# The second layer of a mixture of experts as three products of split fp32r operands

## The reference

```python
xt = x.reshape(-1, d)                       # 4096 tokens, d = 256
route_prob = softmax(xt @ Wr + br)          # 8 experts
routes = argmax(route_prob)
for e in range(8):                          # a token keeps the result of its own expert
    h = gelu(xt @ W1[e] + b1[e])            # 256 -> 1024, exact GELU
    y = h @ W2[e] + b2[e]                   # 1024 -> 256
    out += y * (routes == e)[:, None]
```

## Time and profile before

| | us |
|---|---|
| median of 3 runs | 1250.32 |
| the three runs | 1249.89, 1250.32, 1256.76 |
| span of the profiled execution, first to last instruction | 1249.6 |
| TensorE busy (products) | 1141.2 |
| VectorE, ScalarE, GpSimd busy | 665.9, 424.2, 570.6 |

### The profile page before, as it was taken

One profiled execution on the slowest core, in us unless ns is written; L12 is line 12 of the kernel. 1 busy time (PEld: TensorE's weight loads), 2 busy tenths in 40 slices (PEclk: granted clock), 3 DMA queues, 4 the chain that ended last, 5 costly groups with the idle time before them and its releaser, 6 DMA issues. The chain is left out here.

```text
span 1249.6 us, 23166 instructions
## 1 busy us (share of the span) xinstructions
PE 1141.2 (91%) x7476; PEld 811.9 (65%) x7477; DVE 665.9 (53%) x1481; ACT 424.2 (34%) x501; POOL 570.6 (46%) x565
## 2 busy tenths in 40 slices
PE   6899999897679999999999999998726999999995
PEld 3577677575345555555555555556615999999994
DVE  3264636444557777777777777734751333333331
ACT  1302231311115555555555555563520111111110
POOL 0003030110217888888877787860262444444443
PEclk8899999898689999999999999998957999999998
DMA  7204351304151223232232323233445556556551
GB/s 208 60 1 126 129 175 61 126 34 168 68 188 41 94 64 102 71 98 77 76 92 60 93 59 93 60 119 113 160 113 181 192 195 214 189 192 214 194 191 61
DMA packets 61607, 148.42 MB, mean 119 GB/s; under 512 B 11360, under 2 KB 31776, under 8 KB 59904
## 3 DMA queue, kind: packets, MB, share of 16 engines
q1 hardware_dynamic: 53184, 123.39, 31.0%
q0 software_dynamic: 7536, 22.96, 5.7%
q10 hardware_dynamic: 848, 1.58, 0.5%
HBM read 104.58 MB, written 39.87 MB: 116 GB/s over the span
## 5 line engine op out<-in xcount | busy, mean ns | idle before, releaser
L217 DVE TENSOR_REDUCE s_nmax<-ps_v 128x1 f32<-128x512 f32 x484 | 311.5, 685 | 114.5 <-PE ps_v L211 104.6
L923 POOL TENSOR_TENSOR h_added<-h_added,h_expd 128x1024 f32<-128x1024 f32 x124 | 295.5, 2383 | 37.5 <-ACT h_expd L946 29.6
L946 ACT ACTIVATE h_expd<-ps_v 128x1024 f32<-128x1024 f32 x128 | 131.2, 1025 | 154.9 <-PE ps_v L972 150.3
L1669 PEld LDWEIGHTS ps_h<-xs_c,lnt 128*128 128x128 f32 x1248 | 148.0, 195 | 4.8 <-issue 2.9
L1669 PE MATMUL ps_h<-xs_c,lnt 128*128 128x128 f32 x1248 | 148.4, 278 | 2.3 <-DVE xs_c L1621 2.3
L1679 PE MATMUL ps_y<-w,vals_t 128*128 x624 | 141.2, 379 | 0.6 <-DVE ys L1634 0.6
L418 POOL TENSOR_TENSOR a_res<-a_res,a_lnt 128x2048 f32<-128x2048 f32 x4 | 18.2, 4538 | 266.2 <-DVE a_lnt L123 266.2
L986 PE MATMUL h_ps_o<-h_expd,s_vh 128*32 128x256 f32 x2048 | 137.2, 385 | 0.0
L946 ACT ACTIVATE h_expd<-h_ps_e 128x1024 f32<-128x1024 f32 x128 | 130.3, 1018 | 0.0
L580 PE MATMUL a_ps_v<-a_val,a_expd 128*128 128x257 f32 x512 | 123.4, 396 | 5.1 <-ACT a_expd L458 4.5
L1710 ACT ACTIVATE vals_t<-ps_h 128x1024 f32<-128x1024 f32 x39 | 39.9, 1024 | 255.6 <-DVE ps_h L1614 255.6
(11 more groups left out here) (208 smaller groups left out, 1530.5 us busy)
## 6 DMA issues: line engine op xcount, KB each, us to landing
lnt<-in_w SPq DMA_DIRECT2D x38, 1024.0 KB, 4.9
qk_scr<-a_head_hi SPq DMA_DIRECT2D x16, 512.0 KB, 2.7
qk_scr<-a_head_lo SPq DMA_DIRECT2D x16, 512.0 KB, 3.6
w<-in_w SPq DMA_DIRECT2D x8, 1024.0 KB, 5.5
xs<-xs_scr SPq DMA_DIRECT2D x39, 128.5 KB, 2.1
a_x_t<-in_x_t POOLq DMA_DIRECT2D x4, 1024.0 KB, 9.8
r_scr<-a_res POOLq DMA_DIRECT2D x4, 1024.0 KB, 5.5
v_scr<-res SPq DMA_DIRECT2D x4, 1024.0 KB, 3.9
```

The costliest lines, as they stand in the source:

```text
L217: self.nc.vector.tensor_reduce(self.nmax[k][:, nb, half:half + 1], ps_m[:, half, :], AX.X, ALU.max, negate=True).then_inc(self.v_max, 1)
L923: nc.gpsimd.tensor_tensor(total[:, :], (expd[:, 0, :] if m == 1 else total[:, :]), expd[:, m, :], ALU.add).then_inc(g_add, 1)
L946: nc.scalar.activation(expd[:, m, :], flat(ps_e[m % 2]), ACT.Exp, scale=SCALE).then_inc(a_exp, 1)
L1669: last = nc.tensor.matmul(ps_h[k][:, c // 4, c % 4 * P:(c % 4 + 1) * P], w1_now[k][:, t, c * P:(c + 1) * P], xs_c[:, t, :], start=(t == 0) ...
```

## The change

Only the expert stage computes differently. The units (GELU's outputs) and the second layer's weights are each split into a part rounded to fp32r and the rest, also of type fp32r. The second layer is then three products for each of 8 blocks: rounded units by rounded weights, rounded units by the weights' rest, and, last, the units' rest by the rounded weights; the product of the two rests is left out. These are 24 fp32r products with 256 columns in place of 8 fp32 products.

The new steps are: ScalarE rounds the units (Copy of 128 × 1024, right behind GELU) and the weights of the tile's expert (Copy of 128 × 2048, two tiles ahead); VectorE subtracts to get the weights' rest (128 × 2048, one tile ahead, behind the bias) and the units' rest (128 × 1024, behind the result). ScalarE also takes over the token copy from VectorE. TensorE reads the split weights at fixed places, so it no longer loads the expert's number; VectorE and ScalarE load it once more a tile. The wait for the second layer's weights moves from TensorE to ScalarE. New buffers (`hid_t`, `hids`, `w2s`) need room, so some that end with the routing stage are allocated so that they can be freed.

```diff
--- before.py
+++ after.py
@@ -1419,7 +1419,9 @@
 
         w1_now = [keep["lnt"][:, :, :].rearrange("p t c -> p (t c)")[:, k * CT * H:(k + 1) * CT * H].rearrange("p (t h) -> p t h", h=H)
                   for k in range(2)]
-        hid_t = [keep["vals_t"][:, k, :, :] for k in range(2)]
+        hid_t = [sb(f"hid_t{k}", [P, KC, P]) for k in range(2)]
+        hids = [[sb(f"hid_{x}{k}", [P, KC, P], F32R) for x in ("hi", "lo")] for k in range(2)]
+        w2s = [[sb(f"w2_{x}{k}", [P, KC, C], F32R) for x in ("hi", "lo")] for k in range(2)]
         ys = sb("ys", [P, C])
 
 
@@ -1436,9 +1438,9 @@
         g_pause, padded = sem("g_pause"), sem("padded")
         v_step, v_pad, v_start = sem("v_step2"), sem("v_pad"), sem("v_start")
         w1_in = [sem(f"w1_in{k}") for k in range(2)]
-        v_experts, v_xs, v_biased, v_rows, v_ys = sem("v_experts"), sem("v_xs"), sem("v_biased"), sem("v_rows"), sem("v_ys")
+        v_experts, v_biased, v_rows, v_ys = sem("v_experts"), sem("v_biased"), sem("v_rows"), sem("v_ys")
         pe_xs, pe_hid, pe_ys = sem("pe_xs"), sem("pe_hid"), sem("pe_ys")
-        a_gelu = sem("a_gelu")
+        a_gelu, a_xs, a_hid, a_w2, v_hid, v_w2 = (sem(n) for n in ("a_gelu", "a_xs", "a_hid", "a_w2", "v_hid", "v_w2"))
 
         all_consts = 16 * len(TABLE_CONSTS)
 
@@ -1615,10 +1617,20 @@
                                             b1_t[:, bass.ds(e, 1), :].rearrange("p o (k n) -> p (o k) n", n=1).to_broadcast([P, KC, P]),
                                             ALU.add).then_inc(v_biased, 1)
 
-                def tokens(i):
-
-                    dve.wait_ge(pe_xs, i + 1)
-                    nc.vector.tensor_copy(xs_c[:, :, :], ps_x[:, 0:C].rearrange("p (t n) -> p t n", t=CT)).then_inc(v_xs, 1)
+                def weights_lo(i, k):
+
+                    e = expert(i)
+                    dve.wait_ge(a_w2, i + 1)
+                    nc.vector.tensor_tensor(w2s[k][1][:, :, :].rearrange("p k n -> p (k n)"),
+                                            w2[:, bass.ds(e, 1), :, :].rearrange("p o k n -> p (o k n)"),
+                                            raw(w2s[k][0][:, :, :].rearrange("p k n -> p (k n)")), ALU.subtract).then_inc(v_w2, 1)
+
+                def units_lo(i, k):
+
+                    dve.wait_ge(a_hid, i + 1)
+                    nc.vector.tensor_tensor(hids[k][1][:, :, :].rearrange("p k n -> p (k n)"),
+                                            hid_t[k][:, :, :].rearrange("p k n -> p (k n)"),
+                                            raw(hids[k][0][:, :, :].rearrange("p k n -> p (k n)")), ALU.subtract).then_inc(v_hid, 1)
 
                 def result(i, first=False):
 
@@ -1636,21 +1648,21 @@
                 def tile(i, parity=0, first=False, next_tile=True, ahead=True):
                     if next_tile:
                         biased(i + 1, 1 - parity)
-                    if ahead:
-                        tokens(i + 2)
+                        weights_lo(i + 1, 1 - parity)
                     result(i, first)
+                    if next_tile:
+                        units_lo(i + 1, 1 - parity)
 
                 dve.wait_ge(v_experts, 1)
                 dve.wait_ge(bias_in, 32)
-                tokens(0)
+                weights_lo(0, 0)
                 biased(0, 0)
-                tokens(1)
+                units_lo(0, 0)
                 tiles(dve, tile)
 
             @block.tensor
             def _(pe):
                 pe.wait_ge(consts_in, all_consts)
-                pe.wait_ge(sems["w_in"], 16 * E)
 
                 def tokens(i):
                     pe.wait_ge(xs_in, 16 * i + 16)
@@ -1663,7 +1675,7 @@
                     pe.wait_ge(w1_in[k], 16 * nth)
                     if not first:
                         pe.wait_ge(a_gelu, i - 1)
-                    pe.wait_ge(v_xs, i + 1)
+                    pe.wait_ge(a_xs, i + 1)
                     for c in range(KC):
                         for t in range(CT):
                             last = nc.tensor.matmul(ps_h[k][:, c // 4, c % 4 * P:(c % 4 + 1) * P], w1_now[k][:, t, c * P:(c + 1) * P],
@@ -1671,14 +1683,16 @@
                     last.then_inc(pe_hid, 1)
 
                 def second_layer(i, k, first=False):
-                    e = pe.value_load(texp_i[0:1, bass.ds(i, 1)], min_val=0, max_val=E - 1)
                     if not first:
                         pe.wait_ge(v_ys, i)
-                    pe.wait_ge(a_gelu, i + 1)
+                    pe.wait_ge(a_hid, i + 1)
+                    pe.wait_ge(v_w2, i + 1)
                     for c in range(KC):
-                        last = nc.tensor.matmul(ps_y[:, 0:C], hid_t[k][:, c, :],
-                                                w2[:, bass.ds(e, 1), c, :].rearrange("p o n -> p (o n)"),
-                                                start=(c == 0), stop=(c == KC - 1))
+                        for part in range(2):
+                            nc.tensor.matmul(ps_y[:, 0:C], hids[k][0][:, c, :], w2s[k][part][:, c, :], start=(c + part == 0), stop=False)
+                    pe.wait_ge(v_hid, i + 1)
+                    for c in range(KC):
+                        last = nc.tensor.matmul(ps_y[:, 0:C], hids[k][1][:, c, :], w2s[k][0][:, c, :], start=False, stop=(c == KC - 1))
                     last.then_inc(pe_ys, 1)
 
                 def tile(i, parity=0, nth=1, first=False, next_tile=True, ahead=True):
@@ -1707,17 +1721,43 @@
                     if not first:
 
                         act.wait_ge(pe_ys, i - 1)
-                    nc.scalar.activation(hid_t[k].rearrange("p k n -> p (k n)"), flat(ps_h[k]), ACT.Gelu).then_inc(a_gelu, 1)
+                    nc.scalar.activation(hid_t[k][:, :, :].rearrange("p k n -> p (k n)"), flat(ps_h[k]), ACT.Gelu).then_inc(a_gelu, 1)
+                    act.wait_ge(a_gelu, i + 1)
+                    nc.scalar.activation(hids[k][0][:, :, :].rearrange("p k n -> p (k n)"),
+                                         hid_t[k][:, :, :].rearrange("p k n -> p (k n)"), ACT.Copy).then_inc(a_hid, 1)
+
+                def tokens(i):
+
+                    act.wait_ge(pe_xs, i + 1)
+                    nc.scalar.activation(xs_c[:, :, :].rearrange("p t n -> p (t n)"), ps_x[:, 0:C], ACT.Copy).then_inc(a_xs, 1)
+
+                def weights_hi(i, k, first=False):
+
+                    e = act.value_load(texp_i[0:1, bass.ds(i, 1)], min_val=0, max_val=E - 1)
+                    if not first:
+
+                        act.wait_ge(pe_ys, i - 1)
+                    nc.scalar.activation(w2s[k][0][:, :, :].rearrange("p k n -> p (k n)"),
+                                         w2[:, bass.ds(e, 1), :, :].rearrange("p o k n -> p (o k n)"), ACT.Copy).then_inc(a_w2, 1)
 
                 def tile(i, parity=0, first=False, next_tile=True, ahead=True):
+                    if ahead:
+                        tokens(i + 2)
                     if next_tile:
                         gelu(i + 1, 1 - parity, first)
+                    if ahead:
+                        weights_hi(i + 2, parity)
 
                 pad_rows(act, range(E // 2, E))
                 act.wait_ge(scattered, 16 * (TB - NB))
                 act.wait_ge(v_experts, 1)
                 e0 = act.value_load(texp_i[0:1, 0:1], min_val=0, max_val=E - 1)
                 act.dma_start(w1_now[0], io["w1"][bass.ds(e0, 1)].rearrange("o (t p) m -> p (o t) m", p=P)).then_inc(w1_in[0], 16)
+                act.wait_ge(sems["w_in"], 16 * E)
+                weights_hi(0, 0, first=True)
+                weights_hi(1, 1, first=True)
+                tokens(0)
+                tokens(1)
                 gelu(0, 0, first=True)
                 tiles(act, tile)
 
@@ -1738,18 +1778,19 @@
...
-        keep["token_id"] = ctx.enter_context(nc.sbuf_tensor("token_id", [P, TB], I32))
+        for n, shape in (("vals_t", [P, B * CT, NB, P]), ("res1", [P, NB, C]), ("vals_c", [P, CT, N])):
+            keep[n] = until_experts.enter_context(nc.sbuf_tensor(n, shape, F32))
         head_phase(nc, io, keep, sems, heads)
         during_heads.close()
-        keep.update(kept((("lnt", [P, TB, C + 1]),)))
-        keep["pos"] = ctx.enter_context(nc.sbuf_tensor("pos", [P, TB], I32))
+        keep["lnt"] = ctx.enter_context(nc.sbuf_tensor("lnt", [P, TB, C + 1], F32, side="right"))
         output_phase(nc, io, keep, sems)
         until_experts.close()
         expert_phase(nc, io, keep, sems)
```

More of the change, by code:

```diff
@@ L1740, in program @@
             "pe_vt", "pe_pr", "a_vt", "res_in0", "res_in1", "res_in2", "res_in3", "table_in", "bias_in")}
-        keep.update(kept((("w2", [P, E, KC, C]), ("padding", [P, C + 1]), ("vals_t", [P, B * CT, NB, P]),
-                          ("res1", [P, NB, C]), ("w_pr", [P, CT, C]), ("w_rt", [P, CT, D]), ("b_rt", [P, E]),
+        keep.update(kept((("w2", [P, E, KC, C]), ("padding", [P, C + 1]), ("w_pr", [P, CT, C]), ("w_rt", [P, CT, D]), ("b_rt", [P, E]),
                           ("prior", [P, TB + 1, E]), ("b1_t", [P, E, KC]), ("before", [P, P]), ("allones", [P, P]),
```

(4 more changed lines are left out.)

## The result

The changed kernel takes 1289.06 us (median of 4 runs, 1286.75 to 1291.56), the one before 1250.11 in the same session (4 runs, 1248.88 to 1256.76): ratio 1.0281, interval 1.0254 to 1.0308, so 2.8% slower.

A forecast was written before the change was run, and what follows sets the result against it. TensorE bounded the kernel at 7.24 us a tile; GpSimd's loop was to take over at 6.24 + 0.95 + 1.0 = 8.2. Intervals +35 and +1, start -1: +35 on 1249.6, plus 0.7, 1285 us; range 1220 to 1300.

The forecast's parts named there:

- the loop with both waits: Expert stage: GpSimd's hold and gather both wait for VectorE's subtractions; loop 8.2 us a tile, 1285 us, chance 50%.
- The hold behind the units' rest: GpSimd's first hold after a result waits for VectorE's units' subtraction: +0.95 us a tile.
- The gather behind the weights' rest: GpSimd's gather issue, at 3.4 us after a result, waits for VectorE's weights' subtraction until 4.4: +1.0 us a tile.
- only the first wait: Rival: the hold waits but DMA issues pass; loop 7.2 us a tile, 1249 us; only one wait, 13%.
- The scatter: GpSimd's scatter clears the weights' subtraction by 0.2 us; rival, it is caught: loop 9.5 us, 1334 us, chance 12%.
- The rival bound by TensorE: Expert stage: GpSimd's waits don't happen, TensorE stays the bound; 1225 us (1218 to 1234), chance 25%.
- TensorE's products: Second layer: 24 fp32r products at 117 ns take 2.81 us, so TensorE's tile needs 6.60 us, 0.64 less.
- ScalarE and VectorE: Expert stage: 4.3 us a tile on ScalarE, 5.6 on VectorE, both below TensorE; no added table loads priced.
- The start: Start of the expert stage: second tile's token copy no longer behind the first bias addition; about -1 us, at most 1.23.
- who ends TensorE's idle time: Expert stage: TensorE idle 1.6 us a tile, ended by the result on VectorE.
- hidden, with 0.6 us left: First-layer weights land 12.6 us after an earlier first layer's start and are wanted at 13.2, so cost nothing.

The follow-up runs named there:

- e3: Changed kernel with the units' subtraction reading GELU's output from PSUM and the weights' subtraction reading zeros from PSUM: 1232.68 us, 0.9841 of the kernel before.
- e1: Changed kernel with only the units' subtraction reading GELU's output from PSUM instead of SBUF: 1256.37 us, 1.0024 of the kernel before.
- e2: Changed kernel with only the weights' subtraction reading zeros from PSUM as its second input: 1245.90 us, 0.9945 of the kernel before.
- e5: Changed kernel with the units' subtraction reading PSUM and SP loading first-layer weights before tokens: 1287.36 us, 1.0277 of the kernel before.
- e6: Changed kernel with both subtractions left out, still 24 products: 1230.79 us, 0.9822 of the kernel before.
- e4: Changed kernel with SP loading a tile's first-layer weights before its tokens: 1289.15 us, 1.0288 of the kernel before.
- e7: Changed kernel with the weights' subtraction issued twice in a row: 1307.27 us (one run).
- e8: Changed kernel with the weights' subtraction in four pieces and the units' in two, all inputs in SBUF: 1256.52 us, 1.0041 of the kernel before.
- e10: Changed kernel with the units' subtraction reading PSUM and the weights' subtraction in four pieces: 1238.18 us, 0.9882 of the kernel before.

## Why the prediction was right

The forecast (1285, the loop with both waits) came within 4 us of 1289.06, and with its mechanism: the loop is 8.22 us where 8.2 was forecast. That 1289 lies in the stated range, 1220 to 1300, says little, as the range held the TensorE-bound case and no change too; the loop and the two waits, measured one by one, say more.

- **The hold behind the units' rest:** +0.95 forecast, 0.88 by the last interval, 0.90 by the hold itself. e3 and e1 take the wait away by moving one input to PSUM, so its cause is shown.
- **The gather behind the weights' rest:** +1.0 forecast, 1.10 by the intervals, 1.17 by the issue itself (2.15 for 0.98); e2 takes it away. The 0.86 us between the end of the subtraction and that of the issue stood in the earlier trace rows already: 0.85 at 931.74, 0.84 at 920.80. The Trainium skill (SBUF — State Buffer, "Who interferes with whom") has the rule that such instructions keep out GpSimd's reads, and e3 agrees, with 1.10 us back to 0.196. Its remark that subtractions of this kind were not seen to stall DMA issue doesn't carry over to this gather, whose issue goes from 0.98 to 2.15 us and back. The gather is indirect and takes its indices from the SBUF column `id_in`; whether that reading is what waits, no run separates from the rest of the issue. The rival built on it, only the first wait, had the right price for what e2 then made (7.08 for the 7.2 I gave it), but not for the change.
- **Their sum** came out, but not as a sum of two costs. The hold alone costs 0.8 us (e2), the gather's wait alone 1.9 to 2.0 (e5), and both together 2.0. I had computed the second wait as what is left from 3.4, the gather's start with the hold's wait in it, to 4.4, the end of the weights' rest; so the hold's 0.95 cancels, and what counts is that end, 4.4 forecast and 4.46 measured. The range of the forecast case, which let each wait vary by itself, had this wrong; it did no harm.
- **The scatter** clears the weights' rest in every tile (no issue over 1.02 us), by 0.34 us in the timeline above for the 0.2 forecast. It then runs 0.67 us beside the weights' rest without being stretched: only its start had to come first. The first interval is long for another reason: 9.1 us, as the gather there starts 0.14 us behind the weights' rest (967.85 and 967.71) and takes 3.01.
- **The rival bound by TensorE** (1225) was well priced and its condition was wrong: e3 and e6, in which GpSimd's waits are gone, take 1233 and 1231, and scaled by their ratios to the 1250 us of the kernel before 1230 and 1228.
- **TensorE's products** pass 120 ns apart (1106.46 and 1106.58), not 117, so the second layer takes 2.88 us instead of 2.81, and its tile 6.67 (6.64 to 6.69 in e6 and e3) instead of 6.60. The term was 0.07 us too small, without effect on the change, where TensorE isn't the bound; over 38 tiles it is 2.7 of the 3 us by which e6, scaled so, misses the rival's 1225.
- **ScalarE and VectorE** as forecast: 1.90, 1.06 and 0.38 us (1.88, 1.02, 0.38), 2.28 and 1.22 (2.31, 1.23). No table load was added: one in the expert stage, as before.
- **The start** was to bring 1 us. The first result starts at 964.27 for 964.21; the second layer of the first tile did start earlier (959.74 for 960.56), but its result stands behind the second bias and the weights' rest and gives that back. This is the same queue order that I had priced for the later tiles and had left out here.
- **Wrong: who ends TensorE's idle time.** I forecast the result on VectorE, and had the first layer's weights "hidden, with 0.6 us left". They land late in 35 tiles. The step that failed took the 5.9 us from result to weights' issue over from the kernel before, though both waits stand between the two: counted from the same point, the result's end, it is 7.8 us in the timeline above (1105.57 to 1113.38). It cost nothing, as e4 shows: with the weights in time TensorE waits for the tokens instead.

The sum, as measured: 36 intervals grew from 7.24 to 8.23 (+35.6), the first from 7.25 to 9.1 (+1.9), the last from 6.24 to 7.12 (+0.9), and the start brought nothing: 38.4 us, where +35 was forecast. The first interval, the start and 0.03 us a tile make the difference.

## What to carry to other kernels

Before an arithmetic instruction with two SBUF inputs is added to VectorE, look for what GpSimd reads of SBUF, its DMA issues included, in the time that it will run, and charge each with the rest of that instruction if GpSimd stands on a loop. Two such waits in a row need not add up: where the second ends at a fixed place in VectorE's queue, the first is hidden in it. The remedy is cheap where one input is in PSUM anyhow, or where the instruction can be cut: the wait is for the piece that runs. And where two in-order queues meet like this, a fraction of a microsecond decides which goes first, so the sum of two improvements can be worse than either (e1 with e4).

## What the runs showed that was not expected

- GpSimd gets in between two such VectorE instructions that follow each other at once: e7's gather passes between two of 2.28 us, and e8's waits are bounded by a piece (653 ns for 179 for a copy, with pieces of 684).
- The loop depends on the order of SP's loads with the same arithmetic: e1 (8.2 and 6.7 us in turn, 7.36 on average) and e5 (8.14) differ in that order alone, and loading the weights earlier made the kernel 2.5% slower (1.0277 for 1.0024).
- A gather can be late without any wait at its issue: in e1 its rows landed after a 1 MB load that had been issued about a microsecond before it, 4.3 to 4.9 us after the gather's start instead of 2.7 to 3.2.
- Cutting a subtraction costs little: four pieces of 683 ns overlap at their ends, and four of them stand as 2.48 us in e10's timeline, against 2.28 for the whole.
